# A vision tower's first phase: TensorE's program written out for all its steps, with the other engines left in their loops

## The reference, cut to what matters

```python
# tokens: every 4x4 patch is one token; a query from its mean attends over its 16 pixels
q = _ln(reduce_feats, ln_q_w, ln_q_b) @ Wq.T
kv = _ln(unf, ln_kv_w, ln_kv_b) @ Wkv.T
attn = softmax(einsum('bhpd,bhpnd->bhpn', q * scale, k))
h = reduce_feats + aggre @ proj_w.T + proj_b
# attention in chunks of 128 tokens, 8 heads of 8 channels, with a decay by distance
scores = einsum('bhcd,bhed->bhce', qi, ki) * mask
S_new = blk * S + einsum('bhcd,bhce->bhde', ki * k_dec, vi)
h = _layernorm(h + o @ w_proj + b_proj)
# 8 experts, the best 2 per token
h = _layernorm(h + moe(h))
```

## Time and profile before

| | us |
|---|---|
| median of three runs | 2736.36 |
| the three runs | 2732.22, 2736.36, 2746.99 |
| the profiled execution, its own time | 2729.64 |
| span of that execution | 2727.9 |
| TensorE busy in it | 2346.9 (86%) |
| DVE, ACT, POOL busy | 1952.6, 1897.0, 1830.5 (72%, 70%, 67%) |

### The profile page before, as it was taken

One profiled execution on the slowest core, in us unless ns is written; L12 is line 12 of the kernel. 1 busy time (PEld: TensorE's weight loads), 2 busy tenths in 40 slices (PEclk: granted clock), 3 DMA queues, 4 the chain that ended last, 5 costly groups with the idle time before them and its releaser, 6 DMA issues. The chain is left out here.

```text
span 2727.9 us, 93705 instructions
## 1 busy us (share of the span) xinstructions
PE 2346.9 (86%) x32965; PEld 1104.8 (40%) x32965; DVE 1952.6 (72%) x4552; ACT 1897.0 (70%) x4717; POOL 1830.5 (67%) x1949
## 2 busy tenths in 40 slices
PE   2788888888888888888888888888888986999997
PEld 1344444444444444444444444444444443333332
DVE  3576767776666677777676766776667776899987
ACT  3777777777777777777777777777777773555554
POOL 3687777777777777777777777777777762232233
PEclk9999999999999999999999999999999997999999
DMA  4333333333232333333333333333333300000001
GB/s 87 67 64 64 64 64 64 64 64 63 60 62 57 63 64 64 64 64 64 64 64 64 64 64 64 64 64 64 64 64 64 63 2 1 20 20 19 19 19 28
DMA packets 573783, 148.94 MB, mean 55 GB/s; under 512 B 573440, under 2 KB 573440, under 8 KB 573440
## 3 DMA queue, kind: packets, MB, share of 16 engines
q1 hardware_dynamic: 573440, 143.52, 26.7%
HBM read 135.09 MB, written 8.39 MB: 53 GB/s over the span
## 5 line engine op out<-in xcount | busy, mean ns | idle before, releaser
L704 POOL TENSOR_TENSOR pv<-vs,aw 128x512 f32<-128x512 f32 x512 | 535.4, 1078 | 433.4 <-DVE aw L918 433.4
L586 ACT ACTIVATE xd<-xb 128x512 f32<-128x512 f32 x512 | 575.3, 1149 | 0.0
L380 PE MATMUL ps<-xb,w_ckv 64*64 64x512 f32 x2048 | 559.3, 623 | 7.6 <-DVE kqs L835 6.0
L385 PE MATMUL ps<-xb,w_ckv 64*64 64x512 f32 x2048 | 559.5, 623 | 0.0
L835 DVE TENSOR_TENSOR kqs<-ps,qqT 128x512 f32<-128x512 f32 x512 | 352.3, 688 | 288.7 <-PE ps L385 283.9
L568 ACT ACTIVATE sqs<-ps 128x512 f32<-128x512 f32 x512 | 311.1, 608 | 156.8 <-PE ps L385 156.6
L846 DVE TENSOR_TENSOR sm<-ps,decay 128x1024 f32<-128x1024 f32 x256 | 301.6, 1220 | 135.8 <-PE ps L462 135.0
L857 DVE TENSOR_REDUCE agg<-pv 128x128 f32<-128x1024 f32 x128 | 252.5, 1973 | 172.2 <-POOL pv L711 172.2
L748 POOL TENSOR_TENSOR xt<-xb 128x512 f32<-128x512 f32 x256 | 325.3, 1271 | 21.7 <-issue 21.3
L481 PE MATMUL ps<-sm,vpad 128*32 128x128 f32 x4096 | 191.2, 282 | 171.7 <-DVE kqs L835 151.7
L711 POOL TENSOR_TENSOR pv<-pv 128x512 f32<-128x512 f32 x256 | 321.7, 1278 | 0.0
(11 more groups left out here) (213 smaller groups left out, 4319.4 us busy)
## 6 DMA issues: line engine op xcount, KB each, us to landing
xb<-in_x_dram SPq DMA_DIRECT2D x512, 256.0 KB, 4.3
out_dram<-outb SPq DMA_DIRECT2D x128, 64.0 KB, 1.6
w1p<-in_L_ffn_w_dram SPq DMA_DIRECT2D x16, 16.0 KB
w2p<-in_L_ffn_w_dram SPq DMA_DIRECT2D x8, 16.0 KB
b1p<-in_L_ffn_b_dram SPq DMA_DIRECT2D x8, 0.2 KB
sm<-in_L_tok_Wkv_dram SPq DMA_DIRECT2D x4, 16.0 KB, 2.0
w_av<-in_L_attn_w_qkv_dram SPq DMA_DIRECT2D x4, 16.0 KB, 2.0
b2v<-in_L_ffn_b_dram SPq DMA_DIRECT2D x4, 2.0 KB
```

Of the source, the lines that this page charges most:

```text
L380: nc.tensor.matmul(KB[own, :], w_ckv[own, 2 * P + m * C:2 * P + (m + 1) * C], xv[own, j], start=True, stop=True)
L385: mm = nc.tensor.matmul(CB[(1 - m) * C:(2 - m) * C, :], w_ckv[own, m * C:(m + 1) * C], xv[own, j], start=True, stop=True)
L586: nc.scalar.activation(xd[:, j, :].rearrange("p (b t) -> p b t", b=ST), xb[:, f, :].rearrange("p (b t d) -> p d b t", b=ST, d=ST)[:, j], A ...
L704: nc.gpsimd.tensor_tensor(pv[:, at].rearrange("p (k d) -> p k d", d=D), vs[:, s, at].rearrange("p (k d) -> p k d", d=D), aw[:, j * W4:(j + ...
```

## The change

A second function beside `units` calls `step` for all units in Python, with no `Fori`, and TensorE's program of phase 1 uses it. ACT, POOL, DVE and SP are as they were.

```diff
@@ -72,6 +72,11 @@
             for r in range(4):
                 step(i, r)
         for u in range(UNITS - 4, UNITS + 6):
+            step(u // 4, u % 4)
+
+    def unrolled(eng, step):
+
+        for u in range(-2, UNITS + 6):
             step(u // 4, u % 4)
 
     with ExitStack() as ctx:
@@ -539,7 +544,7 @@
                     projected()
                     attended()
                     state()
-                units(pe, step)
+                unrolled(pe, step)
 
             @block.scalar
             def _(act):
```

## The result

| | before | changed |
|---|---|---|
| median, us | 2734.29 (4 runs) | 2671.53 (4 runs) |
| lowest and highest | 2728.39, 2746.99 | 2667.51, 2679.64 |
| profiled execution, span | 2727.9 | 2677.9 |

The changed kernel takes 0.9765 of the time (95% interval 0.9741 to 0.979): 62.8 us faster, where 97 were forecast. The profiled execution is the slowest of its four; its span is 50.0 us shorter than that of the one profiled before.

What follows compares the result with a forecast made beforehand. It took TensorE, busy 86%, to be delayed by 28 loop returns in phase 1, within a round through DVE and POOL. 28 × 3.49 = 97.7 us, taken as 97: 2736.4 − 97 = 2639 us, range 2616 to 2664.

Steps and rivals of the forecast that it cites:

- The stand is the code's reload at the return: TensorE's 28 issue waits at line 345, 80.8 us, were put to fetching code when phase 1's loop goes back.
- A return costs 4.56 us less 1.07 us of slack: At each TensorE loop return, 2.91 us stand plus 1.65 us clock, less slack: 3.49 us, times 28 is 97.7 us.
- the 1.65 us of low clock: Extra time of the matmuls from line 345 behind a return, at a granted clock of 0.63 on average.
- The steps ahead of the loop are a fair model: Eight return-free steps before phase 1's loop, 65.59 us per four, were taken for all 29 passes: 96.9 us gained.
- the rival of the falling clock: TensorE's clock still drops once in four steps without returns; 46 us stay, 2685 us at most; chance 0.03.
- The two estimates: Gain from removing TensorE's loop, by the cost of 28 returns (97.7 us) and by the stretch of 29 passes (96.9 us).
- Register arithmetic and the longer program cost nothing: On TensorE in phase 1, removed register work gains nothing and about 232 blocks of straight code are fetched ahead: cost 0.
- The DVE's return, taken at 0: The DVE's phase 1 loop return, hidden behind a 4.68 us wait, was priced at 0, with 2.91 us as upper bound.
- ACT's two gathers: ACT's gathers around its loop return stand as one run of 2.13 us, read as showing that its return costs nothing.
- What would show it: Signs in the later profile: no issue waits, clock 1.00 in the old loop's stretch, kqs waits summing to some 190 us.

Runs made afterwards that it cites:

- Experiment 4: Kernel before, loop kept, with half as many matmul instructions in the value projections, each computing 128 columns instead of 64: 2694.40 us (one run).
- experiment 1: Changed kernel plus three constant matmuls per TensorE step, just ahead of the wait for the DVE's keys in attend; the attention's sum is altered: 2638.58 us.
- experiment 5: Changed kernel plus three constant matmuls per step inside the stand in attend, added so that the attention's sum stays whole: 2640.02 us.
- experiment 6: As experiment 5, on the changed kernel, but with one added matmul per step inside the stand instead of three: 2636.68 us.
- Experiment 11: As experiment 6, with the DVE's loop of phase 1 written out as well, ACT and POOL keeping theirs: 2655.57 us.
- experiment 7: As experiment 5, with ACT, POOL and DVE written out as well in phase 1: 2649.81 us.
- experiment 10: As experiment 6, with ACT and POOL written out as well, the DVE keeping its loop: 2628.36 us.
- experiment 9: Changed kernel plus three constant matmuls per step ahead of keys(3), behind the stand in attend: 2721.25 us (one run).
- experiment 12: Changed kernel plus one constant matmul per step ahead of keys(3), behind the stand in attend: 2688.98 us.
- experiment 8: Kernel before, loop kept, with 32 very small matmuls run once in the written-out steps of units 4 to 7, shifting the loop in TensorE's program: 2699.23 us.

## Why the prediction was wrong, point by point

**The stand is the code's reload at the return: right.** Of 28 issue waits none is left. Experiment 4 keeps the jumps and shortens the code, and the waits go.

**A return costs 4.56 us less 1.07 us of slack: right as what a return like the one I read costs, wrong as what goes with it, and this is the step that failed.** The 18 returns with a fall only at them cost 3.66 us (3.49 said), and all that stood above the undisturbed stretch was 93.6 us (97 said). But the 1.65 us of low clock in the sum came from one return, and I took it 28 times as something that the return causes and that goes with it. That part, 28 × 1.65 = 46 us, was nearly all kept: 10 of the 29 falls in the trace of before were not at a return, and with the returns gone there were 27 falls behind the stand in `attend`, 38.7 us.

**The steps ahead of the loop are a fair model: right for the steps, wrong for the clock.** 65.6 to 65.7 us is what four undisturbed steps take in the changed kernel and in experiments 1, 5 and 6. That the clock stays up in them was read from one of the two windows; the other, 94.34 to 159.78, says 0.97 in the earlier trace rows, and there was no return in it. The fall in it comes behind the wait of 2.3 us at line 380 in the earlier trace rows, while the pipeline fills; experiment 6, where no usual stand brings a fall, has it too. So it did not speak of the stand in `attend`, but it did show that the clock falls without a return, and I set the rival of the falling clock to 0.03. The mechanism and its price were in that rival, which kept at most 46 us; 38.7 us were left in the profiled execution, and less in the faster ones, whose mean clock is 0.973 to 0.976 where the profiled one has 0.970. The two estimates agreed, 97.7 and 96.9, because both took the clock to stay up once the returns were gone.

**Register arithmetic and the longer program cost nothing: right.** The matmuls at the steps' borders follow each other as before, no issue wait above 0.2 us stands in the stretch, and 258 blocks of code were loaded in place of 318, 228 of them in the stretch (232 said). The sequencer does run ahead: the records of the branch lie 1.7 to 2.5 us ahead of the end of TensorE's work in the kernel before.

**The DVE's return, taken at 0: right in effect.** Experiment 11 removes it and the stretch does not get shorter. What other returns do cost, about 5 us, is ACT's or POOL's (experiments 7 and 10), which I had dismissed because ACT's two gathers stood side by side.

**What would show it:** no issue waits, and the wait at line 486 in each step, summing to 192.5 us over the span (190 said): seen. The clock of 1.00 in the stretch: not seen, and this was the sign named for the rival.

Left open: what beside the stand decides in which steps the clock falls (experiments 4, 9 and 12), where the other 5 us of experiment 10 come from, and whether moving the DVE's loop of phase 2 in its program would save what experiments 7 and 11 lost there, which was not tried.

## What to carry to other kernels

Before pricing what follows a stall, count it over the whole trace: a low clock found behind one stall may also come behind another, and will then still be there when the first is gone. A hardware loop was cheap here while its body was held (a branch of 0.21 us, hidden behind the matmuls) and cost 1.9 to 2.9 us of stand a return once it was not, and then the position of the loop in the code mattered. Where the matrix engine waits for the others in every step, one matmul added in the wait can pay: here 35 us of 2671.

## What the runs showed of the hardware that was not expected

- One added 128x128 matmul a step, inside a stand of 1.56 us, took the falls of TensorE's clock from 27 to 0 and the median from 2671.5 to 2636.7 us; the same matmul outside the stand left 19.
- Code that runs once moved the median of a kernel by 1.4% (experiment 8): the loop's end then lies elsewhere in its block of code, and the reload, 1.6 to 2.2 us beside another fetch, takes 0.9 to 1.3 us alone.
- Writing out the DVE's program of phase 1 slowed phase 2 by 12 to 16 us, five stands at the returns of a loop that was not edited. The reloads show in queue 14, which holds the code of the engines other than TensorE in blocks of 8 KB; queue 8 holds TensorE's, in blocks of 16 KB.
